# Sparsemax cross-attention with a mixture of experts, one core: the attention loop's body from six items to twelve

## What is computed

```python
def sparsemax(x):
    x = x - jnp.max(x, axis=-1, keepdims=True)
    zs = -jnp.sort(-x, axis=-1)
    ...
    return jnp.clip(x - tau, 0.0)
qh = _split_heads(q @ Wq + bq)
kh = _split_heads(k @ Wk + bk)
vh = _split_heads(v @ Wv + bv)
scores = jnp.einsum('bhqd,bhkd->bhqk', qh, kh) * scale
attn = sparsemax(scores)
out = jnp.einsum('bhqk,bhkd->bhqd', attn, vh)
...
x = x + jnp.tanh(g_xattn[0]) * _L0_xattn_ref(_layernorm(x, axis=-1), ctx_1024, ctx_1024, ...)
x = x + jnp.tanh(g_ffn[0]) * _L0_ffn_ref(_layernorm(x, axis=-1), ...)
```

## Time and profile before

| | |
|---|---|
| median of 3 runs | 7035.43 us (7033.51 to 7036.8) |
| the profiled execution | 7039.05 us, span 7037.1 us, granted clock 0.73 |
| busy, share of the span | DVE 5965.4 us (85%), ACT 5620.4 us (80%), PE 5172.3 us (74%), POOL 2481.6 us (35%) |
| DMA | 417.56 MB, mean 59 GB/s |

### The profile page before, as it was taken

One profiled execution on the slowest core, in us unless ns is written; L12 is line 12 of the kernel. 1 busy time (PEld: TensorE's weight loads), 2 busy tenths in 40 slices (PEclk: granted clock), 3 DMA queues, 4 the chain that ended last, 5 costly groups with the idle time before them and its releaser, 6 DMA issues. The chain is left out here.

```text
span 7037.1 us, 168443 instructions
## 1 busy us (share of the span) xinstructions
PE 5172.3 (74%) x20066; PEld 1710.6 (24%) x20067; DVE 5965.4 (85%) x50050; ACT 5620.4 (80%) x12612; POOL 2481.6 (35%) x10299
## 2 busy tenths in 40 slices
PE   8985776776777777676767777776777777779794
PEld 5551111111111111111111111111111111158573
DVE  4558999999999999999999999999999999945445
ACT  2327998998999999998999999989999999922231
POOL 2222333333333333333333333333333333323431
PEclk9996676776677666676666676766676676789897
DMA  5761111111111111111111111111111111154235
GB/s 194 237 205 44 31 31 30 32 31 29 31 32 31 31 31 31 30 29 31 31 28 30 32 33 31 32 30 28 34 32 31 34 32 32 25 183 176 90 100 187
DMA packets 370269, 417.56 MB, mean 59 GB/s; under 512 B 118688, under 2 KB 286240, under 8 KB 368672
## 3 DMA queue, kind: packets, MB, share of 16 engines
q1 hardware_dynamic: 355872, 370.61, 18.7%
q0 software_dynamic: 13056, 35.74, 1.4%
HBM read 249.13 MB, written 156.88 MB: 58 GB/s over the span
## 5 line engine op out<-in xcount | busy, mean ns | idle before, releaser
L871 DVE MAX8 a_cand<-a_scores 128x8 f32<-128x42 f32 (+1 forms) x38912 | 4386.0, 195 | 297.2 <-issue 255.3
L594 PE MATMUL a_ring<-a_q,a_k 99*128 99x512 bf16 (+1 forms) x3328 | 1470.1, 554 | 799.8 <-ACT a_scores L659 533.6
L624 ACT ACTIVATE a_junk_act<-a_cand,a_ntau 128x304 f32<-128x304 f32 (+1 forms) x3840 | 1932.2, 518 | 150.9 <-DVE a_ntau L733 65.4
L539 PE MATMUL a_out<-a_attn,a_v 128*16 128x512 f32 (+1 forms) x6656 | 1407.1, 787 | 524.2 <-ACT a_attn L663 524.0
L659 ACT COPY a_scores<-a_ring 128x1024 f32<-128x1024 f32 (+1 forms) x2048 | 1607.6, 827 | 205.9 <-DVEq L825 107.8
L663 ACT ACTIVATE a_attn<-a_ring 128x1024 f32<-128x1024 f32 (+1 forms) x1792 | 1653.1, 975 | 2.0 <-PE a_ring L594 1.6
L590 PE MATMUL a_ring<-a_k,a_q 96*128 96x512 bf16 (+1 forms) x4096 | 1345.4, 457 | 83.2 <-DVE a_ident L684 32.9
L624 ACT ACTIVATION_READ_ACCUMULATOR a_junk_act<-a_cand,a_ntau 128x1 f32 x3840 | 784.9, 204 | 0.0
L590 PEld LDWEIGHTS a_ring<-a_k,a_q 96*128 96x128 bf16 x4096 | 385.9, 117 | 1454.4 <-ACT a_attn L663 673.4
L594 PEld LDWEIGHTS a_ring<-a_q,a_k 99*128 99x128 bf16 (+1 forms) x3328 | 285.7, 118 | 1642.3 <-ACT a_scores L659 913.7
L539 PEld LDWEIGHTS a_out<-a_attn,a_v 128*16 128x16 f32 (+1 forms) x6656 | 136.4, 100 | 1203.3 <-ACT a_attn L663 755.5
(11 more groups left out here) (227 smaller groups left out, 6279.1 us busy)
## 6 DMA issues: line engine op xcount, KB each, us to landing
a_k<-k_parts SPq DMA_DIRECT2D x1536, 50.0 KB
k_parts<-p_ks SPq DMA_DIRECT2D x48, 800.5 KB, 7.4
o_parts<-a_o SPq DMA_DIRECT2D x1024, 32.0 KB, 1.6
e_o<-o_parts SPq DMA_DIRECT2D x64, 512.0 KB
p_ctx<-in_ctx_t SPq DMA_DIRECT2D x16, 1601.0 KB, 8.6
v_heads<-p_v SPq DMA_DIRECT2D x16, 1536.0 KB
a_q<-q_parts SPq DMA_DIRECT2D x1536, 16.0 KB
a_v<-v_heads SPq DMA_DIRECT2D x256, 96.0 KB
```

The costliest lines, as they stand in the source:

```text
L539: mm = nc.tensor.matmul(out_ps[at:at + HEAD_DIM], v_st[0:rows, u, c], attn[0:rows, k, (c % 2) * BANK:(c % 2 + 1) * BANK], start=c < 4, sto ...
L594: mm = nc.tensor.matmul(at[0:rows, m * BANK:(m + 1) * BANK], k_st[0:SCORE_ROWS + TAU_ROWS, ut, c * P:c * P + rows], q_st[0:SCORE_ROWS + TA ...
L624: ins = nc.scalar.activation(into[:, t].rearrange("p (a b) -> p a b", b=CHUNKS), cand[:, u % SLOTS, t, 0:w], ACT.Relu, bias=ntau[:, u % 2, ...
L871: ins = V.max(cand[:, u % SLOTS, t, :, c], scores[:, u % SLOTS, t, lo:hi])
```

## The change

A constant LONG = 2 * U = 12 takes U's place in `walk` and in PE's three parts. The straight-line part ahead of the loop has twelve steps, the loop's body has twelve, and the loop runs over `range(1, 21)`: items 12 to 251 in 20 bodies. The tail is as before, items 252 to 259. The slot is still i % 6, and PE's g is now `g * 2 + n // 6`. SP's code is not changed.

```diff
@@ attend_program
     N = BATCH * HEADS
     U = 6
+    LONG = 2 * U
     SLOTS = 3
...
     def walk(engine, step):
 
-        for i in range(U):
-            step(i, i)
-        with engine.Fori(1, N // U) as g:
-            for u in range(U):
-                step(g * U + u, u)
-        for i in range(N // U * U, N + LAG + 1):
+        for i in range(LONG):
+            step(i, i % U)
+        with engine.Fori(1, N // LONG) as g:
+            for n in range(LONG):
+                step(g * LONG + n, n % U)
+        for i in range(N // LONG * LONG, N + LAG + 1):
             step(i, i % U)
...
-            for i in range(U):
-                step(i, i, 0)
-            with pe.Fori(1, N // U) as g:
-                for u in range(U):
-                    step(g * U + u, u, g)
-            for i in range(N // U * U, N + LAG + 1):
+            for i in range(LONG):
+                step(i, i % U, i // U)
+            with pe.Fori(1, N // LONG) as g:
+                for n in range(LONG):
+                    step(g * LONG + n, n % U, g * (LONG // U) + n // U)
+            for i in range(N // LONG * LONG, N + LAG + 1):
                 step(i, i % U, i // U)
```

## The result

Twelve items per body take **6963.3 us** (median of 5 runs, 6962.4 to 6968.9) against 7035.4 us before: a ratio of 0.990, 95% interval 0.989 to 0.991, 72 us less. The forecast was 6991.4 us (44 us less), its range 6985 to 7010. The direction was right, the size was not, and the result lies 28 us under the forecast and 22 us under the range: some 30 us or more came from something that the prediction left at nothing.

A forecast was written before the change was run, and what follows sets the result against it. The prediction took DVE to bound the attention loop, with ACT following. 21 fewer DVE jumps at 2.1 us gave 44.1 us, all other terms 0, so 7035.4 - 44 = 6991.4 us, range 6985 to 7010.

The forecast's parts named there:

- Point 1: DVE's loop back jumps: 21 of 40 go, at 2.1 us each, saving 44.1 us.
- point 4: Longer stretches without a jump: ACT, at 20.34 us per item against DVE's 20.6, keeps up; 0, other bound 33 us.
- The 0.73 us hole ahead of the 40 MAX8: DVE's idle gap at the test whether tiles are unsettled: claimed to be in every item and to stay.
- point 3: Items 6 to 11 moved to straight-line code ahead of the loop: same work per item, cost 0, at most 1 us.
- The lower end of the range: 6985 us: half way from 44 us saved to the 57 us that 21 jumps of 2.7 us could at most give.
- Point 2: Jumps of ACT, POOL and PE, which go with DVE's: nothing more counted, as DVE sets the time.
- ACT becomes a second bound: Rival on stretches without a jump: ACT limits the items; 7024 us with all 33 us, 7008 with half; chance 0.09.
- Point 5: The remaining 19 jumps: a longer body might change their cost by 4 us either way; taken as 0.
- Point 6: PE's doubled body, some 1650 instructions, may be refetched, a hole of 2.5 to 2.7 us at 19 jumps, covered: 0.
- slower rival: PE fetches several packets before going on; a hole of 8.5 us costs 70 us against 44 saved: 7062 us; chance 0.04.
- the cover of 4.8 us: PE's slack at the loop jump, 3.8 + 1.0 us, from waiting for ACT's a_attn and making the score piece early.
- Point 7: SP's loop still steps by six with its 2.5 us jump; loads run six items ahead, so nothing.

The follow-up runs named there:

- before_shift128: The kernel before, with DVE's code shifted by 128 instructions by a never-entered `While` of 124 increments ahead of it; 7039.4 us, ratio 1.000.
- long_shift56: The changed kernel (bodies of twelve) with 56 semaphore increments ahead of DVE's attention code; 6998.5 us, ratio 0.995 to the kernel before.
- before_shift64: The kernel before, with DVE's code shifted by 64 instructions by a never-entered `While` of 60 increments ahead of it; 6997.7 us, ratio 0.994.
- others_long: The kernel before with bodies of twelve on PE, ACT and POOL only, DVE staying at six; 7042.7 us, ratio 1.001.
- dve_alone_long: The changed kernel with twelve items per body on DVE only, PE, ACT and POOL at six; 6972.4 us, ratio 0.9905 to the kernel before.
- half_out_copy: The changed kernel with ACT's output copy cut from 512 columns to 64, leaving out the rest of the output; 6953.8 us.
- long_head_late: The changed kernel with DVE's code shifted by a never-entered `While` of 106 increments, putting its loop head 7 instructions ahead of a border; 6992.0 us.
- dve_shift40: The kernel before with 40 semaphore increments ahead of DVE's attention code, bodies still of six; 7065.5 us, ratio 1.004.

## Why the prediction was wrong in its size

The runs cross the two causes. Sum of the 255 item steps, us:

| | 41 bodies of six | 20 bodies of twelve |
|---|---|---|
| tests dear | before 5585.8; before_shift128 5584.8 | long_shift56 5544.3 |
| tests cheap | before_shift64 5554.7 | after 5515.0 |

Fewer jumps bring 41.5 us along the upper row and 39.7 along the lower one; the cheaper tests bring 30 us (5584.8 - 5554.7) along the left column and 29 us along the right one. That both ways agree is what the table shows: the two causes add up. Any way through it gives the 70.8 us. (In `long_shift56` 43 of the 218 tests were cheap all the same, so the upper row flatters the jumps by some 6 us.)

The table is made of one profiled execution per kernel, and that of `before_shift64` lay 11.5 us above its median. The medians give 35 to 41 us for the tests (`long_shift56` to the change, before to `before_shift64`) and 34 to 40 us for the jumps; of the 35 us, 5 lie ahead of the first item (571.6 against 566.6 us), where `long_shift56` executes its 56 increments. So the tests are worth 30 to 41 us and the jumps 34 to 40 us, about half of the gain each.

Of the 31 us between before and `before_shift64` in the table, 13 lie in the 37 steps that enter the `While` (27.41 to 27.05 us on the mean), 6 in the 36 steps that hold a jump and don't enter it (22.77 to 22.61) and 11 in 177 plain ones (20.62 to 20.56). So the whole 0.34 us by which the hole shrank comes through in the steps with a general solution, and only 0.06 us in a plain one. That DVE has fallen behind the other engines in the first and is held by them in the second fits ACT's 107 us of waits for these steps, but is argued.

- **Point 1, jumps, 44.1 us: right in mechanism and count, a tenth or more too large.** 21 jumps went, each with the hole forecast. They measured 34 to 40 us, 1.6 to 1.9 each. That a little of the freed time goes into other waits (point 4) is argued.
- **"The 0.73 us hole ahead of the 40 MAX8 is in every item (the test whether tiles are unsettled) and stays": this is the step that failed.** It didn't stay. With point 3, "Work per item is the same on each engine", it put the price of moved code at nothing. The instructions are the same, but a skip that crosses a border every 128 instructions costs 0.46 us instead of 0.14, and the change moved all tests of the loop off these borders. Of 0.34 us in each of 216 items, 73 us, some 30 to 41 reached the total; the new wait for POOL took up to 30 more, and the rest stays open. The lower end of the range fell with it, as it allowed only for dearer jumps.
- **Point 2, the others' jumps, nothing: right while DVE's stand (`others_long`).** With DVE's gone they are worth 4 to 9 us at most, within the intervals (`dve_alone_long`). In the table whatever they are worth is part of the jumps' share.
- **Point 4, ACT keeps up: right for the 44 us.** DVE's rows of waits that name ACT hold 37.4 us in the change and held 38.5; nearly all of them are holes of a jump. The wait for POOL grows only with the cheap tests: it is 4.6 us in `long_shift56`, 32.1 us in the change. Beyond the forecast's gain something else does hold DVE back, but the rival "ACT becomes a second bound" has it only in part: time freed on ACT alone gave 10 us (`half_out_copy`).
- **Point 5, 0 +- 4 us: right here by luck.** A longer body by itself made the jumps no dearer, but the place of its head can: the heads of before and after lie well, and in `long_head_late` 19 jumps cost 29 us more, 1.5 each.
- **Point 6, PE: right, and its slower rival wrong.** The body of 1662 is kept. Even at 4978, with 3.5 us, the cover of 4.8 us held to within the runs' spread. The prediction weighed two rules of the Trainium skill (Advanced Engine Details and Errata, ISA Cache) for that: the two lines would have had PE fetch in each round, the size of 128 KB not. The rows decide for the size: there is no q8 in the loop at 1662. The same section gives the line as 16 KB or 256 instructions, which the prediction passed over; by two such lines PE's body of some 820 would have been fetched in each round before the change too, and the earlier trace rows show no q8 between 780 and 6050 us.
- **Point 7, SP: right.** No row of DVE's waits names a load.

Both rows that could have told were read: the earlier trace rows showed the 0.73 us as an issue wait, and 262 issue waits stand in the earlier trace rows against 40 jumps. But I took the hole for the price of the test itself, wherever it stands.

## What to carry to other kernels

Where the bounding engine's waits are "for issue", the place of its branches in the instruction stream is part of the cost: an edit that moves code can gain or lose as much as the edit itself. Before such a change is judged, run the old kernel with its code shifted by a skipped block; here that alone was worth 41 us, where the change was worth 72. A longer body gains at most one exposed jump per body saved; here it was 1.6 to 1.9 us of 2.1.

## What the runs showed of the hardware

- A taken forward branch over 45 instructions costs DVE 0.14 us behind the branch (213 tests of the change), or 0.46 us if it crosses one of the borders that recur every 128 instructions (216 tests before). These borders fit the packets: q14 moved 8.63 MB in 1053 packets, 8.2 KB each. The Trainium skill (Runtime: NRT & Kernel Launch, Instruction fetch mechanics) gives blocks of 16 KiB for 256 instructions, so that a packet would be 128, and calls the crossing "mostly hidden". The size per instruction fits; the spacing, half a block, and the exposed 0.3 us do not.
- A loop head 7 instructions ahead of a border costs a second hole of 1.6 us per jump, behind the seventh instruction (`dve_shift40`, `long_head_late`). Heads 3, 11 and 17 instructions behind a border, and 47 (before) and 61 (`long_shift56`) ahead of the next, have the usual jump: their items take 22.6 to 22.8 us. Heads at other small distances ahead of a border weren't tried, and why the borders lie at 64 and not at 0 of my count stays open; that the cause is the fetch itself is argued from the counts, not seen.
- PE keeps a body of 1662 recorded instructions (branch 0.2 us, no q8 in the loop) and refetches one of 4978 (112 packets of q8 between 1500 and 5500 us), for 3.5 us per jump. Nothing between the two sizes was run.
- A taken back jump leaves DVE without an issued instruction for 2.7 to 3.1 us, whether its body holds six items or twelve; 1.9 to 2.1 us of it show as idle time, since some MAX8 are still queued.
